# First attention: norm on ScalarE, expert weights loaded raw by chunks, top values copied once in four tiles; second attention reordered

## The reference

```
x = x + attention0(layernorm(x), ctx)     # 16 heads of 16; q and k normalized in each head
x = x + experts0(layernorm(x))            # 8 experts, the best 2 by softmax; hidden 512
x = x + attention1(layernorm(x), ctx)     # one head of 256: (x_n + softmax(q k) v) @ Wo + bo
x = x + experts1(layernorm(x))            # 32 experts, the best 4; hidden 128; and a shared expert of 512
```

## Time and profile before

| | us |
|---|---|
| time, median of 3 runs | 1439.72 (1438.53 to 1444.93) |
| the profiled execution | 1447.97 |
| its span, from first to last instruction | 1446.1 |
| TensorE busy, of the span | 1322.6 (91%) |
| GpSimd busy | 663.6 (46%) |
| VectorE busy | 766.0 (53%) |
| ScalarE busy | 594.8 (41%) |

### The profile page before, as it was taken

The page is one execution under the profiler, slowest core; times in us unless marked ns, Lnnn a source line. Parts: engine busy times, 40 slices in busy tenths (PEclk is TensorE's granted clock), DMA queues, the critical chain, the costliest instruction groups (busy, mean ns, idle before and its releaser), DMA issues. The chain is left out here.

```text
span 1446.1 us, 29159 instructions
## 1 busy us (share of the span) xinstructions
PE 1322.6 (91%) x7743; PEld 1056.2 (73%) x7744; DVE 766.0 (53%) x1965; ACT 594.8 (41%) x1314; POOL 663.6 (46%) x905
## 2 busy tenths in 40 slices
PE   7998999999879999999999599847999999989993
PEld 4665777777558888888888387724888888858882
DVE  4884888887732222222222488693233333347764
ACT  2455777777322222222222377635333333322110
POOL 1213565665113333333332366504555555257775
PEclk9998999999889999999999599966999999999997
DMA  2108322222731111111111677554455555745554
GB/s 96 59 30 307 114 92 89 78 96 100 288 119 48 50 50 51 50 50 51 51 51 37 202 228 218 163 232 155 154 164 161 162 161 156 131 125 161 161 161 126
DMA packets 117387, 179.94 MB, mean 124 GB/s; under 512 B 17210, under 2 KB 91979, under 8 KB 113996
## 3 DMA queue, kind: packets, MB, share of 16 engines
q1 hardware_dynamic: 80980, 100.29, 20.8%
q0 software_dynamic: 20736, 56.65, 14.6%
q10 hardware_dynamic: 15608, 22.25, 4.3%
HBM read 115.13 MB, written 59.77 MB: 121 GB/s over the span
## 5 line engine op out<-in xcount | busy, mean ns | idle before, releaser
L1228 POOL DMA_INDIRECT xg<-t_xn,token x160 | 151.7, 948 | 157.7 <-PE psum L2093 72.8
L2167 POOL DMA_INDIRECT su_yg<-t_y,slot x128 | 125.4, 980 | 67.9 <-issue 38.1
L2105 PE MATMUL psum<-gu,m_xT 128*128 x640 | 154.2, 384 | 0.0
L1465 PE MATMUL psum<-w,m_hT 128*128 x576 | 136.3, 380 | 0.8 <-ACT m_hT L1384 0.8
L1403 DVE TENSOR_TENSOR m_h<-psum,m_h 128x512 f32<-128x512 f32 x72 | 49.8, 691 | 164.8 <-ACT m_h L1378 164.8
L2105 PEld LDWEIGHTS psum<-gu,m_xT 128*128 128x128 f32 x640 | 117.2, 193 | 13.2
L1444 PE MATMUL psum<-w,m_xT_high 128*128 x288 | 120.8, 420 | 0.0
L2064 DVE TENSOR_TENSOR m_h<-psum,m_sg 128x256 f32<-128x256 f32 x80 | 34.0, 425 | 162.0 <-ACT m_sg L2043 161.9
L1444 PE MATMUL psum<-w,m_xT_low 128*128 x288 | 114.9, 399 | 0.0
L1444 PE MATMUL psum<-w_low,m_xT_high 128*128 x288 | 114.2, 396 | 0.0
L1465 PEld LDWEIGHTS psum<-w,m_hT 128*128 128x128 f32 x576 | 103.8, 190 | 12.4 <-issue 1.2
(11 more groups left out here) (305 smaller groups left out, 3126.1 us busy)
## 6 DMA issues: line engine op xcount, KB each, us to landing
t_y<-m_y SPq DMA_DIRECT2D x80, 256.0 KB, 2.2
w<-in_w SPq DMA_DIRECT2D x8, 1024.0 KB, 11.3
t_x<-at_x SPq DMA_DIRECT2D x64, 128.0 KB, 2.1
t_w_low<-at_low ACTq DMA_DIRECT2D x64, 128.0 KB, 1.7
w_low<-t_w_low SPq DMA_DIRECT2D x8, 1024.0 KB, 13.3
at_yg<-t_y SPq DMA_DIRECT2D x32, 256.0 KB, 3.1
gu<-in_gu ACTq DMA_DIRECT2D x8, 1024.0 KB, 11.9
w<-in_x SPq DMA_DIRECT2D x16, 256.0 KB, 2.8
```

Source lines behind the costliest of these rows:

```text
L1228: pool.indirect_dma_start(out=g.xg1[j % GB][:, k * D:(k + 1) * D], out_offset=None, in_=g.xn4, in_offset=bass.IndirectOffsetOnAxis(ap=g.to ...
L1465: last = pe.matmul(ps_y[:, 0:D], hT[:, c * P:(c + 1) * P], g.w2[:, bass.ds(ex * (MC * D) + c * D, D)], start=(c == 0), stop=(c == MC - 1))
L2105: last = pe.matmul(ps_gu[p][:, k * 2 * M1:(k + 1) * 2 * M1], xT[p][:, at:at + P], g.gu[:, bass.ds(ex[k] * (DC * 2 * M1) + c * 2 * M1, 2 * ...
L2167: pool.indirect_dma_start(out=yg[p][k][:, :], out_offset=None, in_=g.y1, in_offset=bass.IndirectOffsetOnAxis(ap=g.slot[:, at:at + 1], axis ...
```

## The change

In the first attention:

- The norm xn goes from VectorE to ScalarE, at the end of its half (`T_XA` = 8). ScalarE's form needs a shift, -mean x root, which GpSimd computes right behind the root (`ln.shift`, in the second attention this is L148).
- `top_of` writes values and indices into a buffer for four tiles, and these are copied to the router's table once in four tiles.
- w13 isn't loaded up front. SP loads two raw chunks for each tile into the `low` buffers, behind the stores of x1 and xn, after a wait for the store of the low part that was there. ScalarE rounds from `low` into w13's place, once, GpSimd subtracts that from `low` in place, and ScalarE issues the store of `low` at the head of its half instead of the end (`T_STORE` = 10). The second copy of each chunk on ScalarE is gone.

`NS0` is 71: with 8192 pairs, no distribution over 8 experts needs more than 64 + 7 tiles. The experts' loops end one step earlier, with a written-out step behind the loop.

In the second attention the items stand in another order on SP, VectorE, ScalarE and TensorE, TOP goes from 10 to 11, and the router's scores have a PSUM place of their own behind xm's transpose.

```diff
-NS0 = NTOK * K0 // P + E0
+NS0 = NTOK * K0 // P + E0 - 1
...
-        T_HIGH, T_LOW, T_ROUND = 8, 9 + LEAD, 10
-
-        W13_LATE = 3
+        T_HIGH, T_LOW, T_STORE = 8, 9 + LEAD, 10
...
-            def expert_weights(e):
-                n = DC * 2 * M0
-                sp.dma_start(g.w13[:, e * n:(e + 1) * n], g.ins["w13"][:, e * n:(e + 1) * n])\
-                    .then_inc(s_w13 if e else s_w13_first, 16)
+            def weights(i):
+
+                wait(sp, low_st[i.mod(4)], i.div(4).n * 16)
+                sp.dma_start(low[i.mod(4)][:, :].bitcast(F32), g.ins["w13"][:, bass.ds(i.n * CHUNK, CHUNK)])\
+                    .then_inc(s_raw[i.mod(4)], 16)
...
                     sp.wait_ge(x_norm, t.n + 1)
                     sp.dma_start(g.xn[bass.ds(t.n * P, P), :], xn[p][:, :]).then_inc(xn_st[p], 16)
+                t = s.shift(-W13_FROM)
+                if t.within(CHUNKS // 2):
+                    for i in range(2):
+                        weights(t.times(2).shift(i))
...
-                    pool.tensor_tensor(low[i.mod(4)][:, :], chunk(i), low[i.mod(4)][:, :], ALU.subtract).then_inc(w_low, 1)
+                    pool.tensor_tensor(low[i.mod(4)][:, :], low[i.mod(4)][:, :].bitcast(F32), chunk(i), ALU.subtract)\
+                        .then_inc(w_low, 1)
...
                     ln.invert(pool, t)
+                    ln.shift(pool, t)
...
-                    ln.apply(dve, x1[p][:, :], xn[p][:, :], t).then_inc(x_norm, 1)
...
-                    top_of(dve, g, lg[p], top[p], ix[p], t, lg_done, m8_done, ix_done, passed)
+                    at = slice(t.mod(RANKED) * 8, (t.mod(RANKED) + 1) * 8)
+                    top_of(dve, lg[p], top[:, at], ix[:, at], t, lg_done, m8_done, ix_done, passed)
+                    if t.mod(RANKED) == RANKED - 1:
+                        at = bass.ds(t.shift(1 - RANKED).n * 8, RANKED * 8)
+                        dve.tensor_copy(g.top_v[:, at], top[:, :])
+                        wait_alone(dve, ix_done, t.n + 1, passed[0])
+                        dve.tensor_copy(g.top_i[:, at], ix[:, :])
...
             def half(u):
+                i = chunk_at(u, T_STORE)
+                if i is not None:
+                    act.wait_ge(w_low, i.n + 1)
+                    act.dma_start(g.w13_low_d[:, bass.ds(i.n * CHUNK, CHUNK)], low[i.mod(4)][:, :].bitcast(F32))\
+                        .then_inc(low_st[i.mod(4)], 16)
                 i = chunk_at(u, T_HIGH)
                 if i is not None:
-                    wait(act, low_st[i.mod(4)], i.div(4).n * 16)
-                    act.activation(low[i.mod(4)][:, :], chunk(i), ACT.Copy).then_inc(w_high, 1)
+                    act.wait_ge(s_raw[i.mod(4)], (i.div(4).n + 1) * 16)
+                    act.activation(chunk(i).bitcast(F32R), low[i.mod(4)][:, :].bitcast(F32), ACT.Copy).then_inc(w_high, 1)
...
-                i = chunk_at(u, T_ROUND)
-                if i is not None:
-                    act.wait_ge(w_low, i.n + 1)
-                    act.dma_start(g.w13_low_d[:, bass.ds(i.n * CHUNK, CHUNK)], low[i.mod(4)][:, :].bitcast(F32))\
-                        .then_inc(low_st[i.mod(4)], 16)
-                    act.activation(chunk(i).bitcast(F32R), chunk(i), ACT.Copy).then_inc(w_round, 1)
+                t = tile_at(u, T_XA)
+                if t is not None:
+                    p = t.mod(2)
+
+                    wait(act, xn_st[p], t.div(2).n * 16)
+                    wait(act, x_t, t.shift(-1).n)
+                    ln.apply_scalar(act, x1[p][:, :], xn[p][:, :], t).then_inc(x_norm, 1)
...
-        SUM, XA, XN, S, PT, WO, XM, R, TOP = 1, 2, 3, 4, 5, 6, 8, 9, 10
+        SUM, XA, XN, S, PT, WO, XM, R, TOP = 1, 2, 3, 4, 5, 6, 8, 9, 11
```

More of the change, by code:

```diff
@@ L1384, in step @@
                     act.activation(hT[:, :], ps_ht[:, 0:M0], ACT.Copy).then_inc(h_out, 1)
-            steps(act, 4, NS0, NS0 + 2, 2, step)
+            steps(act, 4, NS0 - NS0 % 2, NS0 + 2, 2, step)
         @block.vector
@@ L1410, in step @@
                     dve.tensor_copy(y[p][:, :], ps_y[:, 0:D]).then_inc(y_out, 1)
-            steps(dve, 6, NS0, NS0 + 3, 2, step)
+            steps(dve, 6, NS0 - NS0 % 2, NS0 + 3, 2, step)
         @block.tensor
@@ L1468, in step @@
                     last.then_inc(y_mm, 1)
-            steps(pe, 8, NS0, NS0 + 3, GB, step)
+            steps(pe, 8, NS0 - NS0 % GB, NS0 + 3, GB, step)
 def attention1_phase(nc, g):
@@ L1738, in step @@
                     last.then_inc(s_mm, 1)
-                if (t := stage(s, R)) is not None:
-                    p = t.mod(2)
-                    pe.wait_ge(xm_out, t.n + 1)
-                    pe.wait_ge(exp_done, NT if t.loop is None and t.off + 5 > NT else t.shift(5).n)
-                    pe.matmul(logits_of(t), ones3[:, :], bias3[:, NB * LK:NB * LK + E1], start=True, stop=False)
-                    for c in range(DC):
-                        last = pe.matmul(logits_of(t), xmT[p][:, c * P:(c + 1) * P], wr[:, c * E1:(c + 1) * E1],
-                                         start=False, stop=(c == DC - 1))
-                    last.then_inc(r_mm, 1)
                 if (t := stage(s, XN)) is not None:
@@ L1756, in step @@
                     last.then_inc(x_t, 1)
-                if (t := stage(s, XM)) is not None:
-                    p = t.mod(2)
-                    pe.wait_ge(xm_done, t.n + 1)
-                    wait(pe, xm_out, t.n)
-                    for c in range(DC):
-                        last = pe.transpose(ps_m[:, c * P:(c + 1) * P], xm[p][:, c * P:(c + 1) * P], g.ident[:, :])
-                    last.then_inc(xm_t, 1)
                 if (t := stage(s, WO)) is not None:
@@ L1778, in step @@
                         .then_inc(wo_mm, 1)
+                if (t := stage(s, R)) is not None:
+                    p = t.mod(2)
+                    pe.wait_ge(xm_out, t.n + 1)
+                    wait(pe, lg_done, t.n)
+                    pe.matmul(logits_of(t), ones3[:, :], bias3[:, NB * LK:NB * LK + E1], start=True, stop=False)
+                    for c in range(DC):
+                        last = pe.matmul(logits_of(t), xmT[p][:, c * P:(c + 1) * P], wr[:, c * E1:(c + 1) * E1],
+                                         start=False, stop=(c == DC - 1))
+                    last.then_inc(r_mm, 1)
+                if (t := stage(s, XM)) is not None:
+                    p = t.mod(2)
+                    pe.wait_ge(xm_done, t.n + 1)
+                    wait(pe, xm_out, t.n)
+                    wait(pe, lg_done, t.shift(-1).n)
+                    for c in range(DC):
+                        last = pe.transpose(ps_m[:, c * P:(c + 1) * P], xm[p][:, c * P:(c + 1) * P], g.ident[:, :])
+                    last.then_inc(xm_t, 1)
                 if (t := stage(s, PT)) is not None:
```

114 lines of the change are left out of this document (49 added, 65 removed).

## The result

The changed kernel takes 1461.84 us (median of 4 runs, 1460.33 to 1466.58), the kernel before 1439.81 in the same comparison: ratio 1.0152, 95% interval 1.0132 to 1.0171, so 22 us slower (19 to 25 by the interval). The forecast had been 6 us slower. The profiled execution took 1460.8 us with a span of 1459.0.

What follows compares the result with a forecast made beforehand. TensorE, always busy, was taken to bound the first attention, so only delays beyond the other engines' slack cost time. Terms +15.6 - 1.5 - 5.2 - 2.9 = +6.0 us gave a median of 1446 us, range for 8 in 10 1430 to 1463.

Steps and rivals of the forecast that it cites:

- Attention 0, the weights: First attention: late low-part store and late raw chunk delay TensorE in 13 key batches, +15.6 us, bounds 11.7 to 20.8.
- I take 1.2 us, between the two: First attention: delay per key batch, set between 0.9 (low-part store) and 1.3 (raw chunk load), times 13 batches: 15.6 us.
- the larger one holds: First attention: store delay 0.9 and chunk delay 1.3 us count from the same aggregate, so the larger applies, not their sum.
- the rival of added delays: Follow-up expectation for the first attention: delays add up, so removing the first late half gains 9 us; no chance given.
- The shift's 0.37: First attention, GpSimd: the added shift takes 0.27 us plus about 0.1 to pass its semaphore.
- Tail: End of the first attention (u above 64): 0.4 us saved on three or four tiles, -1.5 us, bounds -4 and +2.
- Slots: Expert loop: 71 slot tiles instead of 72 save one TensorE step, -5.2 us, nothing hides it.
- Attention 1: Second attention: no wait for xm's store, -4.8 us; late expert-row loads, +1.9; together -2.9, bounds -5 and +3.
- R3: Second attention: row loads land 0.3 us too late each step, +7.8 in place of +1.9, 1452 us; chance 0.08.
- R2: First attention: TensorE's clock falls behind 11 of the 13 gaps, +17 us, 1463 us; chance 0.12.
- R1: First attention: the waits are hidden and the 15.6 us goes, -9.6 in all, 1430.1 us; chance 0.22.
- R4: First attention: GpSimd lost a lock to VectorE's norm; without it 5.2 us less, 1440.5 us; chance 0.05.

Runs made afterwards that it cites:

- e5_x_in_last: Changed kernel, but SP loads x last in its step, behind the stores of x1 and xn and the two raw chunks: ratio 1.0058 to the kernel before.
- e6_low_first: Changed kernel, but GpSimd computes the low part ahead of the copy of q and the masked keys: ratio 1.0155 to the kernel before.
- second profile: The kernel before, unchanged, profiled once more: 1437.75 us.
- e3_att1_only: The kernel before with only the second attention of the changed kernel: 1446.43 us, ratio 1.0049.
- e12_norm_on_vector: Changed kernel with the first attention's norm back on VectorE and no shift on GpSimd: 1456.31 us, ratio 1.0111 to the kernel before.
- e7_low_and_xb_first: Changed kernel, but GpSimd computes low part and residual with bias ahead of the copy of q and masked keys: ratio 1.0003 to the kernel before.
- e8_att1_loads_first: The kernel before with the changed kernel's second attention, but SP issues its two loads first in its step: ratio 0.9999.

## Why the prediction was wrong

What bounded the kernel was read rightly. In the first attention TensorE had no slack, so the work taken off VectorE and ScalarE bought nothing, and the order on three other engines decided.

**Attention 0, the weights: right mechanism, price too small.** The steps of the chain are in the changed kernel's rows. GpSimd:

```profile
248.12 0.22 POOL L108 TENSOR_SCALAR at_ln_rstd<-at_ln_mv 128x1 f32<-128x1 f32 x1 [4.94 <-DVE at_ln_mv L137]
...
249.21 0.27 POOL L148 TENSOR_SCALAR at_ln_less<-at_ln_mv,at_ln_rstd 128x1 f32<-128x1 f32 x1 [0.21 <-POOL at_ln_rstd L110]
...
253.23 0.72 POOL L646 TENSOR_TENSOR at_xb<-at_x_in,at_bp 128x256 f32<-128x256 f32 x1
```

SP's queue:

```profile
254.14 0.33 SPq L572 DMA_DIRECT2D at_x_in<-in_x  x1
...
255.19 0.38 SPq L596 DMA_DIRECT2D t_xn<-at_xn  x1
255.87 0.90 SPq L577 DMA_DIRECT2D at_low<-in_w  x2
```

ScalarE:

```profile
253.78 0.42 ACT L719 ACTIVATE w<-at_low 128x256 f32 x1 [2.67 <-POOL at_low L636]
...
258.31 0.42 ACT L719 ACTIVATE w<-at_low 128x256 f32 x1 [1.85 <-DMA at_low<-in_w]
...
259.54 0.70 ACT L731 ACTIVATE w<-w 128x616 f32<-128x616 f32 x1
```

From the root to TensorE's transpose, forecast and measured, in us:

| link | forecast | measured |
|---|---|---|
| root to the end of `xb`, with the shift | 5.76 | 5.83 |
| to SP's load of x | 0.17 | 0.19 |
| to the store of xn | 1.04 | 1.05 |
| to the load of the chunk | 0.45 | 0.68 |
| to ScalarE's copy | 2.20 | 2.44 |
| copy to the end of the exponential | 2.00 | 1.93 |
| to TensorE | 0.10 | 0.06 |
| sum | 11.72 | 12.18 |

The chain was 0.46 longer than forecast, half of it at the chunk's load, which has a wait and an address to compute ahead of it, and half between its issue and the copy. The raw chunks and low stores land after this (min/median/max, 150 to 330 us):

```profile
DMA to landing us min/median/max: 1.7/2.1/3.7
```

The median of both together is the 2.1 that I took, and the chunk loads alone have 2.2. The Trainium skill, page "DMA: Bandwidth & Descriptors", section "Anatomy of one DMA — SWDGE (gpsimd) path", gives about 2.0 us fixed and 436 bytes per ns, an estimate of 2.3 for 128 KB. It is written for transfers that GpSimd issues, the loads here come from SP, and the medians lie 0.1 to 0.2 below it.

Two steps of the prediction failed in size. The link of 0.45, what two issues in a row take here (254.74 to 255.19 between the stores of x1 and xn), was taken for one with a wait and a computed address, which took 0.68. And "I take 1.2 us, between the two" contradicts the sentence ahead of it, "the larger one holds": by its own rule the term was 1.3 x 13 = 17. Measured were 1.69 x 13 = 22.0 by the profiles (above the bound of 1.6), and 19.5 by the runs. The rule itself stood the test: `e5_x_in_last` and `e6_low_first` came out as it says, and the rival of added delays did not. The 19.5 and the 22.0 don't differ clearly, as the runs allow some 3 us. The shift's 0.37 was measured as 0.48: its wait for GpSimd's own root took 0.21, where the prediction had assumed less than the 0.17 between two engines. Its removal gave 5.0 us by the run times and 7.3 in the trace.

**Tail: wrong, small.** From the last score product to the routing's first compare it took 25.7 us, 25.5 before. The -1.5 did not come. (The links listed for it add up to 4.4, not 4.5.)

**Slots: right.** -4.6 against -5.2.

**Attention 1: wrong sign, 6.8 against -2.9.** Both halves of this term were off. The gain was taken as the whole 4.8 us by which the profiled execution was over in 26 steps. The second profile was 1.3 over, so that there was little to gain. I had seen that the profiled execution lay 8.3 us above the median and carried the difference over to the result, as if every execution of the changed kernel would have it too. It was just this execution's excess, and a good part of it stood in the very waits that the term counted, and in the low clock behind them. The cost was the rival R3: the loads have no slack, and here the price was more than its 7.8 - 4.8 = 3.0 net, because the gain was hardly there. Measured were 6.8 by the run times. The prediction's own sum had the second load land at 878.8 and wanted at 879.0, 0.15 in time, and every link in it was a typical one. What came was not a small steady delay. Most steps of `e3_att1_only` keep the pace of 3.30, and single late issues and landings (2.7 to 4.6 us, where 2.8 was taken) stop the stage, at times with the clock falling behind the stop. The profile of before had the sign of it: by its own sum the loads had "no slack", and I gave 8 in 100 to the case that they bind. How a late row reaches TensorE is seen in `e3_att1_only` behind the long issue on SP. VectorE waits for the rows (the row at 884.69 above), the maximum comes behind them, ScalarE's exponential behind that, and TensorE's next transpose is late:

```profile
886.30 0.22 DVE L1642 TENSOR_REDUCE at_nmx<-psum 128x1 f32<-128x77 f32 x1
886.56 0.33 ACT L1711 ACTIVATE at_pr<-psum,at_nmx 128x77 f32<-128x77 f32 x1 [2.63 <-DVE at_nmx L1642]
...
892.21 0.42 PE L1785 MATMUL psum<-ident,at_pr 128*77 128x128 f32 x1
```

**The sum.** 19.5 - 4.6 + 6.8 = 21.7 in place of 6.0. The direction and the first mechanism were right, and the time lay just inside the range of 1430 to 1463, by luck: its upper end stood for the falling clock of R2, which did not come, and the forecast's own range ended at 1453. The size was off by a factor of almost four, by 5.4 us in the first attention with its tail (19.5 for 14.1), 9.7 in the second and 0.6 in the slot. So the step that failed most is the term for attention 1: it booked the waits of one long execution as a gain and gave the loads behind them nearly no price.

**The rivals.** R1 (hidden) is excluded: TensorE has idle time. R2 (the clock falls in the gaps) is excluded for the first attention of the changed kernel, where the clock stayed at 1.00 through 26 stops, the longest of 0.9 us. But what it describes exists. In `e6_low_first` 13 stops of 1.3 to 1.7 us stood in the same stage, and behind two of them, of 1.53 and 1.56, the clock fell. Behind longer ones it did not, so the length of the stop alone doesn't decide. R3 was right as a mechanism. R4 (GpSimd was the loser of a lock) shows next to nothing: with the norm off VectorE, GpSimd's keys took 1217 to 1232 ns each, against the 1220 to 1280 of the earlier trace rows and the 1219 to 1281 of `e12_norm_on_vector`. The exclusive lock that the Trainium skill describes (page "SBUF — State Buffer", section "SBUF: two separate sides") had cost GpSimd at most 0.06 us on such an instruction here, and `e7_low_and_xb_first` has no trace of a gain from it.

## What to carry to other kernels

Where one engine is full, count slack and not busy time. Follow a late value from the place where it is made to the full engine, through every queue in which it stands behind something else, and mind that of several chains from one origin the longest alone is paid. Taking away a shorter one moves the wait and gains nothing, so take them away together: here two items of GpSimd's order, ahead of the long keys, were worth 22 us. And before a stall in a profile is booked as a gain, look whether the profiled execution was itself longer than the median, since a second profile here had only a quarter of it. A loss read from one pair of profiles deserves the same doubt.

## What was not expected of the hardware

- The same kernel took 1520.6 us on one chip and 1439.6 and 1439.3 on two others. Up to the end of the second attention the stages agree. The difference lies behind them, 10 us in the second experts and 70 in the last stage. That stage in the second profile of before, and in `e8_att1_loads_first` on the slow chip:

```profile
1264.00:1436.00 172.00, 150.82 (x624) 118.56 (x622) 107.13 (x224) 29.75 (x64) 124.22 (x128) 0.96 0.50 147
```

```profile
1277.00:1517.00 240.00, 166.36 (x623) 126.88 (x621) 107.71 (x224) 29.74 (x64) 122.91 (x128) 0.86 0.36 105
```

  The work is the same, but the transfers move 105 GB/s instead of 147, and the clock is lower behind the longer waits. In the slow one the profile puts many waits of ScalarE and VectorE, up to 22 us long, down to "remote", which the other doesn't have. Why was not tried.
- Single issues on SP take 0.33 to 0.45 us (0.63 for the store of xm's transpose), but in the second attention of most of these profiles a few take 1.0 to 2.4 us. They fall on another instruction in each execution, often 14 to 21 us apart (in the first profile of before at 813.4, 829.8, 844.4, 861.1 and 880.1). `e3_att1_only` had one of 2.39 at 880.95 us, and the first profile of before one of 1.91 at 880.07. What makes them was not tried. A queue without slack can pay for each of them, and a single profile that is read as typical misleads.
- TensorE's granted clock fell from 1.00 to 0.50 behind stops of 1.53 and 1.56 us in `e6_low_first` and stayed at 1.00 behind stops of 1.58, 1.64 and 1.67 in the same stage. Each fall cost 1.6 us more.
